# Twelve weight transposes set between two back products, an early signal for the turned x, and an exponential in the setup

## What is computed

```python
x = x + tanh(g_xattn[0]) * xattn0(layernorm(x), ctx, mask, ...)   # layer one: layer norms of text and context, softmax, layer norm
x = x + tanh(g_ffn[0])   * ffn0(layernorm(x), ...)                # shared expert + 1 of 8 experts per token
x = x + tanh(g_xattn[1]) * xattn1(layernorm(x), ctx, w1_w, w1_b, w2_w, w2_b)
x = x + tanh(g_ffn[1])   * ffn1(layernorm(x), ...)                # shared expert + 2 of 8 experts per token

def xattn1(bf, kf, w1, b1, w2, b2):
    scores = (bf @ w1.T + b1) @ kf.T / sqrt(256)
    return concat([bf, softmax(scores) @ kf], -1) @ w2.T + b2
```

## Time and profile before

| | |
|---|---|
| times of three runs | 857.18, 859.37, 860.01 us; median 859.37 |
| profiled execution | 860.13 us, of it 858.4 us in the span of the engines |
| PE busy | 825.5 us (96%) |
| DVE, ACT, POOL busy | 376.4, 290.8, 170.2 us |
| TensorE clock granted, mean | 0.997 |

### The profile page before, as it was taken

How to read it: one execution, slowest core, us unless ns; L and a number is a source line. 1 busy time by engine, 2 the same in 40 slices (tenths; PEclk the granted TensorE clock), 3 DMA queues, 4 the chain that set the end, 5 groups by cost and what they waited for, 6 DMA issues and landing times.

```text
span 858.4 us, 12728 instructions
## 1 busy us (share of the span) xinstructions
PE 825.5 (96%) x3892; PEld 585.7 (68%) x3892; DVE 376.4 (44%) x1371; ACT 290.8 (34%) x689; POOL 170.2 (20%) x198
## 2 busy tenths in 40 slices
PE   6999999999999999999989999999999999999996
PEld 6777786666666767676668888765656666666663
DVE  3789988451222222222356666569121121122117
ACT  2677774321122222222134555541022222222220
POOL 4111101222012222211111111021113333333310
PEclk9999999999999999999999999999999999999999
DMA  7466569103000101010274574300001111111108
GB/s 200 108 192 195 178 202 316 67 0 114 19 25 26 37 28 34 31 26 19 72 234 154 175 262 129 129 22 1 19 25 49 44 44 50 44 43 50 44 34 248
DMA packets 49707, 79.13 MB, mean 92 GB/s; under 512 B 6278, under 2 KB 32396, under 8 KB 49644
## 3 DMA queue, kind: packets, MB, share of 16 engines
q1 hardware_dynamic: 25936, 37.91, 14.6%
q10 hardware_dynamic: 17804, 24.91, 8.6%
q0 software_dynamic: 5904, 15.50, 6.0%
HBM read 65.43 MB, written 12.87 MB: 91 GB/s over the span
## 4 chain that ended last, share of the span: by engine, by line
PE 73%; DVE 6%; issue 1%; DMA 1%; ACT 1%; DVEq 0%; SPq 0%; POOLq 0%; ACTq 0%
PE ps L1250 26%; PE ps L1272 14%; PE ps L1162 6%; PE ps L1131 6%; PE ps L1283 4%; PE ps L965 2%; PE ps L1085 2%; PE ps L1017 2%; PE ps L1046 2%; PE ps L1052 2%; PE ps L1226 1%; PE ps L1008 1%; PE ps L1116 1%; PE ps L995 1%; PE ps L1093 1%
## 5 line engine op out<-in xcount | busy, mean ns | idle before, releaser
L1250 PE MATMUL ps<-expert_weights,work 128*128 x280 | 126.1, 593 | 0.3 <-issue 0.3
L1250 PE MATMUL ps<-expert_weights,layer_constants 128*128 x336 | 103.1, 460 | 0.4 <-issue 0.4
L1250 PEld LDWEIGHTS ps<-expert_weights,work 128*128 128x128 f32 x280 | 50.5, 190 | 50.8 <-issue 50.8
L1250 PEld LDWEIGHTS ps<-expert_weights,layer_constants 128*128 128x128 f32 x336 | 62.2, 190 | 31.9 <-issue 0.7
L1786 DVE TENSOR_TENSOR work<-work,ps 128x512 f32<-128x512 f32 x35 | 24.1, 688 | 132.6 <-PE ps L1250 132.6
L1272 PEld LDWEIGHTS ps<-expert_weights,work 128*128 128x128 f32 x280 | 53.1, 190 | 22.7 <-issue 17.3
L1272 PE MATMUL ps<-expert_weights,work 128*128 x280 | 66.2, 379 | 0.8 <-ACT work L867 0.8
L1869 POOL TENSOR_TENSOR x_stream<-x_stream,layer_constants 112x256 f32<-112x256 f32 x32 | 25.0, 782 | 197.1 <-DVE expert_weights L1442 185.5
L1272 PE MATMUL ps<-expert_weights,xn_turned 128*128 x252 | 61.9, 387 | 0.0
L1783 DVE SCALAR_TENSOR_TENSOR xn_turned<-ps,work,xn_turned 128x352 f32<-128x352 f32 x42 | 24.5, 584 | 85.0 <-ACT xn_turned L859 67.4
L1922 POOL DMA_INDIRECT returned<-work,ints x35 | 34.6, 989 | 136.9 <-PE ps L1226 116.8
(11 more groups left out here) (313 smaller groups left out, 1446.0 us busy)
## 6 DMA issues: line engine op xcount, KB each, us to landing
expert_weights<-in_L_ffn_W_dram ACTq DMA_DIRECT2D x24, 512.0 KB, 4.9
work<-in_ctx_dram SPq DMA_DIRECT2D x32, 336.0 KB
expert_weights<-in_L_ffn_w_eDF_dram ACTq DMA_DIRECT2D x8, 704.0 KB, 4.8
expert_weights<-in_L_ffn_w_eDF_dram SPq DMA_DIRECT2D x8, 704.0 KB, 8.8
xn_rows<-expert_weights ACTq DMA_DIRECT2D x32, 112.0 KB, 2.1
work<-returned SPq DMA_DIRECT2D x16, 224.0 KB, 4.7
expert_weights<-mask_rows SPq DMA_DIRECT2D x16, 164.1 KB, 3.6
expert_weights<-in_L_ffn_w_eFD_dram ACTq DMA_DIRECT2D x4, 640.0 KB, 7.0
```

Of the source, the lines that this page charges most:

```text
L1250: ins = mm(ps[:, 2 * half + h, 0:l.FH], m.gT[:, u % 2, k], w.rearrange("p a f -> p (a f)"), start=(k == 0), stop=(k == KD - 1))
```

## The change

Three edits.

The first concerns setup on PE for layer two. It is called from shared_late of layer one, behind the fifth and ahead of the sixth back product, after a wait until all chunk products of layer one's shared expert have been read. The wait for the copies moves to the head of layer two's attention. The wait for shared_read goes from there to L1046 of element 0, the first matmul that writes one of the banks 4 to 7 again.

The second: the two turns of x stand ahead of the wait for the context and carry a signal of their own, xt_turned. ACT's copy to tT waits for that, and the copy to kT for turned. This holds for both layers.

The third: at the end of ACT's setup for layer two stands an exponential of one column into a scratch column (exp_first), which nothing reads.

```diff
@@ act, setup, layer two
                     for h in range(2):
                         nc.scalar.copy(a.w2T[:, 2 * h:2 * h + 2], ps[:, 1 + h, :].rearrange("p (k d) -> p k d", k=KD)
                                        ).then_inc(a.setup_act.sem, 1)
+                    nc.scalar.activation(exp_first[0:T], c0[0:T], ACT.Exp)
@@ act, attention
-                        act.wait_ge(a.turned.sem, a.turned.at(b + 1))
+                        act.wait_ge(a.xt_turned.sem, a.xt_turned.at(b + 1))
                         if due(b):
                             act.wait_ge(a.q_done.sem, a.q_done.at(b))
                         nc.scalar.copy(a.tT, ps[:, 2, 0:KD * T].rearrange("p (k t) -> p k t", k=KD)
...
                     if has(b):
+                        act.wait_ge(a.turned.sem, a.turned.at(b + 1))
                         if due(b - 1):
                             act.wait_ge(a.scores_done.sem, a.scores_done.at(b - 1))
                         nc.scalar.copy(a.kT[:, v % 2], ps[:, 0:KD, 0:S]).then_inc(a.kT_ready.sem, 1)
@@ pe, setup, layer two
                     ins.then_inc(a.setup_pe.sem, 1)
-                    pe.wait_ge(a.setup_act.sem, a.setup_act.at(3))
@@ pe, attention
                 a = A[l.n]
+                if l.n == 1:
+                    pe.wait_ge(a.setup_act.sem, a.setup_act.at(3))
...
                         pe.wait_ge(a.xt_ready.sem, a.xt_ready.at(b + 1))
+                        for k in range(KD):
+                            ins = nc.tensor.transpose(ps[:, 2, k * T:(k + 1) * T], a.xt[0:T, v % 2, k * P:(k + 1) * P],
+                                                      ident[0:T, 0:T])
+                        ins.then_inc(a.xt_turned.sem, 1)
                         if l.n == 0:
                             pe.wait_ge(a.normed.sem, a.normed.at(b + 1))
                         if l.n == 1:
                             landed = a.raw_in[b % KV1]
                             pe.wait_ge(landed.sem, landed.at(32 * (b // KV1 + 1)))
-                        for k in range(KD):
-                            nc.tensor.transpose(ps[:, 2, k * T:(k + 1) * T], a.xt[0:T, v % 2, k * P:(k + 1) * P],
-                                                ident[0:T, 0:T])
...
                             if due(b):
                                 pe.wait_ge(a.xpart_read.sem, a.xpart_read.at(b))
+                            else:
+                                pe.wait_ge(B[0].shared_read.sem, B[0].shared_read.at(NB))
@@ pe, shared_late
+                if l.n == 0:
+                    pe.wait_ge(m.mid_ready.sem, m.mid_ready.at(NB // GT * l.FC))
+                    setup(LAYERS[1])
                 back(l, g, l.FC - 1)
@@ pe, main
+            setup(LAYERS[0])
             for l in LAYERS:
-                setup(l)
-                if l.n:
-                    pe.wait_ge(B[0].shared_read.sem, B[0].shared_read.at(NB))
                 attention(l)
```

More of the change, by code:

```diff
@@ L209, in flamingo @@
         wqbk, qbias, c0 = f.take(KD), f.take(KD), f.take(1)
+        exp_first = f.take(1)
         bqbk = f.take(KD)
@@ L298, in flamingo @@
             a.xb_ready = both_layers("a_xb_ready", l, NB)
+            a.xt_turned = both_layers("a_xt_turned", l, NB)
             a.turned = both_layers("a_turned", l, NB)
```

## The result

The changed kernel takes 851.19 us, median of 13 runs (849.89 to 858.38), beside 858.69 (13 runs, 856.49 to 860.58) for the kernel before: a ratio of 0.9937, 95% interval 0.9918 to 0.9955, 5.4 us. In a second measurement it took 853.08 (6 runs) beside 858.50: 0.9939, 0.9920 to 0.9958. The forecast was 855.7 and the range ended at 853.3, so the direction was right and the gain too small. The profiled execution of after has a span of 848.9 us, 9.5 less than that of before.

What follows compares the result with a forecast made beforehand. PE was taken to set layer two's pace, DVE's dependent chain the middle of layer one's attention, with PE idle 3.8 us at the seam. Start 1.2 plus seam 2.5 (3.5 - 1.0) gave 859.37 - 3.7 = 855.7 us; range 853.3 to 858.3.

Steps and rivals of the forecast that it cites:

- The seam, PE and ACT: Seam of the layers: x part of element 0 earlier 1.6, elements 1 and 2 0.5 and 0.6, exponential 0.8; 3.5 us gained.
- Rival 4: Seam, ACT: the table load takes twice its 1.28 us at its new place; gain 2.4, time 857.0; chance 0.04.
- The late y load: Seam: element 4's y load lands later and may contend with expert weights; 1.0 us taken off, between nothing and 3.8.
- The start of layer one: Layer one's attention: waits ahead of q and part of the context's wait vanish; 1.2 us gained, between 0.5 and 1.9.
- The 0.7 taken off for the half pace: Start of layer one: 1.37 us more work falls into PE's slow time, costing half of it, 0.7 us.
- Rival 1: Seam: the y load lands late enough to eat 2 us and more; 858.6 at the upper end; chance 0.18.
- rival 3: Start of layer one brings nothing because something is fixed; only the seam counts, 856.9; chance 0.04.
- rival 5: Layer two's loop: signal and wait break PE's stream, 0.48 us in each of 16 bodies; slower, 863.4; chance 0.04.
- Rival 2: Layer one: PE reaches full pace before the first scores, which take 1.43, not 2.82; 1.4 more, 854.3; chance 0.08.

Runs made afterwards that it cites:

- e1: Kernel before plus only the moved layer-two setup between the last back products: 855.90 us, ratio 0.9979 to the kernel before.
- e2: Kernel before plus only the early signal for the turned x, in both layers: 856.35 us, ratio 0.9979 to the kernel before.
- e6: Changed kernel without the small exponential, keeping moved setup and early signal: 852.22 us, ratio 0.9925 to the kernel before.
- e8: Changed kernel without the early signal, keeping moved setup and small exponential: 857.73 us, ratio 0.9993 to the kernel before.
- e7: Changed kernel with the y loads of elements 4 and 5 issued earlier by SP: 851.76 us, ratio 0.9931 to the kernel before.
- w2: Changed kernel plus six unread matmuls in PE's wait for layer two's routing table: 850.76 us, ratio 0.9913 to the kernel before.
- e5: Kernel before plus the small exponential and six unread matmuls in PE's wait for the weights' copies: 856.86 us, ratio 0.9982 to the kernel before.
- e3: Kernel before plus only the small exponential at the end of layer two's setup: 861.36 us, ratio 1.0022 to the kernel before.
- w1: Changed kernel plus eight unread matmuls ahead of PE's first wait: 848.93 us, ratio 0.9890 to the kernel before.
- w3: Changed kernel plus unread matmuls, six ahead of PE's first wait and three in the routing table's wait: 848.97 us, ratio 0.9890 to the kernel before.
- w4: As w3, plus three unread matmuls in setup and two ahead of the first context's turns: 847.05 us, ratio 0.9866 to the kernel before.

## Why the prediction fell short

Step by step, with what the runs showed:

- **The seam, PE and ACT: right.** 1.6 + 0.5 + 0.6 + 0.8 = 3.5 was forecast; between the same blocks 1.8 + 0.3 + 0.6 + 0.9 = 3.6 came. The moved setup gives 1.93 (e1) and the signal 1.24 (e2), and with both it is 3.17 (e6), just their sum; the exponential adds 0.77 where the signal is missing (e8 against e1) and 0.44 where it is there (after against e6), since the table load makes the first x part wait 0.57 there, where it had not waited at all (e6), and without the signal only 0.56 instead of 0.43. The table load took the 1.28 of the earlier trace rows at its new place, the exponential 0.20 (0.25 was my estimate), PE's wait 0.57 (0.7). Rival 4 is refuted: the load is over at 433.99, and the exponential starts at 434.00. By the Trainium skill (ScalarE: Activation LUTs, What ACT_TABLE_LOAD costs) a drain would have added 1.38 us; no row here shows one.
- **The late y load, 1.0 off: the step that failed.** My own bookkeeping had DVE's next x at 448.4 and PE wanting it at 448.3, a loss of 0.1, and then I took 1.0 for a contention with the weights. DVE's side came out as worked out, x ready 1.8 us behind the y; but the load landed 5.5 us after its issue (437.09 to 442.6), faster than the 5.9 of the earlier trace rows, although the weights were issued from 439.47 on. e7 shows that nothing is lost. A cost that no row showed was taken off the sum for the sake of its worst case.
- **The start of layer one, 1.2: the mechanism right, the term too small.** From setup's last block to the first scores it is 12.26 or 12.27 in the five profiles without the signal and 10.52 to 10.54 in five with it (after, the second profile, e2, e6, w2): 1.7, where I had 1.3. The 0.7 taken off for the half pace was no mistake: the second scores follow the first by 5.75 to 5.97 without the signal and by 6.05 to 6.34 with it, although the wait of 0.53 between them is gone. So at the second scores 1.3 was left; at the seam's first rows, 411.87 to 412.09 behind setup's last block without the signal and 410.14 to 410.50 with it, it was 1.6. My reading of the earlier trace rows that DVE is the fuller engine in between was wrong: PE is busy 83.07 of 88 us, DVE 79.46. The gain came through all the same.
- **Rival 1** (y load) and **rival 3** (start brings nothing) are refuted by e7 and by the start's rows, **rival 5** by the 6.95 us that a body of layer two keeps. (In rival 1 half of the 3.8 us gives 856.7, not 856.9; nothing hangs on it.) **Rival 2** (full pace sooner) is open. In both profiles of the changed kernel, e2, e6 and w2 the first scores still take 2.82. But in e7 they take 1.50, and it is 407.52 us from setup's last block to the seam, 2.6 less than in the lowest of the five; in the second profile of the changed kernel the q of element 0 ran at full pace too (1.13, with 2.05 in before). None of the five profiles without the signal shows either, and two of six don't tell whether the signal brings it. What the first profile shows, full pace in the second half of setup, comes with and without the edits (e5 and e8 have it, before, e1, e3, e7 and the second profile of the changed kernel don't).
- **The numbers.** 1.6 + 3.6 = 5.2 agrees with both ratios (5.4 and 5.2). The base was 859.37, from three runs; thirteen gave 858.69. So 858.69 - 5.2 = 853.5 would have been the time, close to that of the second measurement (853.08). The first thirteen runs have their median another 2.3 lower: eight lie between 849.9 and 851.4, five between 853.6 and 858.4. The granted clock fits, 0.989 to 0.999 in the eight and 0.986 to 0.988 in four of the five; but two profiles don't show how much of the 2.3 it is, so that part of the gain stays unexplained. My range took in neither the base nor this scatter.

Not foreseen at all was that an edit can cost clock. I had put e3 at no difference, and had the change been made of that part alone, the forecast would have missed a loss.

## To carry to other kernels

Take a transfer's lateness as a cost only as far as the engine that sets the pace will stand for it: follow it to the time when PE wants the result, and keep a contention that no row shows for the range. Compare two profiles only between points where PE ran at the same pace, and read unchanged blocks first: a block that no edit touches and that takes twice as long is the clock, not the change. Parts of a change can be worth less alone than together, when the wait that one part lengthens stands behind a wait that another part removes.

## What the hardware showed

- Behind two waits close together, 1.71 and 0.70 us, the granted clock was 0.50 from 439.9 to 443.4 in the profile of e3; behind 1.71 and 0.43, in before, it stayed at 1.00. In two of e3's twelve runs there was no such stretch.
- The same kernel gets different clocks at the same place in different executions: the second half of setup ran at full pace in one profile of the changed kernel and at half in the other, worth 1.8 us. PE's work ahead of it counts as well: eight matmuls of setup took 1.97 us with the start filled and 3.76 without (w1 and after). The Trainium skill (TensorE: Matmul & The Clock Gate, What's actually happening) says that activity releases the throttle and that the number of slow matmuls at a kernel's start varies from run to run; both agree with these traces.
- Work that nobody needs, put into PE's waits, made the changed kernel about 0.5% (w1, w3) to 0.7% (w4) faster by the ratios.
